# Cross-attention average of a decoder layer: values as stationary 32-column weights in four column groups, divisors by a ones product

## What is computed

```
k, v  = split((ctx @ W_src.T + b_src) * mask)         # ctx: 128 x 512 per sequence
q     = (x1 @ W_tgt.T + b_tgt) * mask                 # 8 heads of 32 channels
attn  = softmax(where(mask, q @ k.T / sqrt(32), -inf))
upd   = attn @ v
x2    = layernorm(x1 + concat([x1, upd]) @ W_out.T + b_out)
```

## Time and profile before

| | us |
|---|---|
| median of three runs | 1570.22 |
| the profiled execution's own time | 1569.91 |
| its span in the trace | 1568.2 |
| PE busy in the span | 1355.5 |
| DVE busy in the span | 915.1 |
| ACT busy in the span | 689.8 |
| GpSimd (POOL) busy in the span | 541.7 |
| `attend`: first weight DMA issued at | 673.01 |
| `attend`: last copy of logits at | 1051.81 |
| `attend`: busy PE from 693.73 to 1014.81, of 321.08 | 314.06 |

### The profile page before, as it was taken

The page is one execution under the profiler, slowest core; times in us unless marked ns, Lnnn a source line. Parts: engine busy times, 40 slices in busy tenths (PEclk is TensorE's granted clock), DMA queues, the critical chain, the costliest instruction groups (busy, mean ns, idle before and its releaser), DMA issues. The chain is left out here.

```text
span 1568.2 us, 24828 instructions
## 1 busy us (share of the span) xinstructions
PE 1355.5 (86%) x8188; PEld 1035.6 (66%) x8189; DVE 915.1 (58%) x1735; ACT 689.8 (44%) x1253; POOL 541.7 (35%) x460
## 2 busy tenths in 40 slices
PE   4889556669999999569999999969979999999995
PEld 1344456658888888358888888855756666666653
DVE  4899759769999999535454445446512212122196
ACT  2545349947777777323433343331022222222214
POOL 2565500014555555522312331211234444444311
PEclk9999878889999999679999999979989999999998
DMA  3698787744333332042232021023021111111164
GB/s 89 149 244 234 207 221 198 216 121 104 95 94 94 94 94 61 14 123 71 85 98 98 31 62 61 28 81 110 0 74 54 57 57 55 56 56 57 59 200 134
DMA packets 147325, 158.20 MB, mean 101 GB/s; under 512 B 63440, under 2 KB 112176, under 8 KB 145712
## 3 DMA queue, kind: packets, MB, share of 16 engines
q1 hardware_dynamic: 134320, 123.63, 27.0%
q0 software_dynamic: 8320, 29.37, 7.3%
q10 hardware_dynamic: 4608, 4.20, 0.8%
HBM read 104.72 MB, written 42.99 MB: 94 GB/s over the span
## 5 line engine op out<-in xcount | busy, mean ns | idle before, releaser
L2531 DVE TENSOR_TENSOR hidden<-unit_psum,gate 128x352 f32<-128x352 f32 x72 | 37.8, 525 | 210.1 <-ACT gate L2494 210.1
L1944 POOL TENSOR_TENSOR scores<-scores,score_max 128x1024 f32<-128x1024 f32 x32 | 60.8, 1899 | 243.2 <-DVE score_max L1872 243.2
L478 PE MATMUL proj_psum<-filtered 128*128 128x512 f32 x192 | 96.0, 648 | 34.8 <-DMA filtered<-in_xT 28.1
L2462 PE MATMUL unit_psum<-wd,hiddenT 128*128 (+1 forms) x432 | 112.0, 395 | 14.2 <-issue 12.9
L549 PE MATMUL proj_psum<-window,toep 128*128 128x128 f32 x512 | 77.2, 319 | 46.8 <-DMA toep<-in_fir 24.3
L2393 POOL DMA_INDIRECT unit_rows<-x_rows,token_of_slot x72 | 69.8, 970 | 126.9 <-PE unit_psum L2436 104.4
L668 ACT ACTIVATE filtered<-proj_psum 32x512 f32<-32x512 f32 x168 | 98.6, 587 | 30.3 <-PE proj_psum L549 26.3
L549 PEld LDWEIGHTS proj_psum<-window,toep 128*128 128x128 f32 x512 | 73.4, 231 | 50.5 <-issue 47.6
L697 DVE SCALAR_TENSOR_TENSOR filtered<-proj_psum,conv_taps,filtered 128x508 f32<-128x508 f32 (+1 forms) x144 | 95.0, 733 | 19.3 <-ACT filtered L596 19.3
L2400 POOL DMA_INDIRECT outs<-unit_out,choice_of_slot x72 | 71.1, 987 | 99.8 <-DVE unit_out L2536 97.1
L2462 PEld LDWEIGHTS unit_psum<-wd,hiddenT 128*128 128x128 f32 (+1 forms) x432 | 76.4, 190 | 37.0 <-issue 29.1
(11 more groups left out here) (286 smaller groups left out, 3258.5 us busy)
## 6 DMA issues: line engine op xcount, KB each, us to landing
toep<-in_fir SPq DMA_DIRECT2D x32, 384.0 KB, 4.0
neg_decay_blocks<-in_gw1s POOLq DMA_DIRECT2D x8, 1280.0 KB, 10.6
ndg<-filtered SPq DMA_DIRECT2D x8, 1024.0 KB, 6.1
neg_decay_gram<-ndg SPq DMA_DIRECT2D x16, 512.0 KB, 3.7
ctxT_tiles<-in_ctxT SPq DMA_DIRECT2D x16, 512.0 KB, 3.6
gathered<-outs SPq DMA_DIRECT2D x32, 256.0 KB, 3.0
window<-value SPq DMA_DIRECT2D x32, 192.0 KB, 4.0
filtered<-in_xT SPq DMA_DIRECT2D x8, 512.0 KB, 7.0
```

The source lines that it names most:

```text
L478: mm = pe.matmul(psum[:, pair_bank(n, p, m % 2), :], wqkv[m // KD][:, k, (m % KD) * 128:(m % KD) * 128 + 128], xT[:, u, k, :], start=(k == ...
L1944: pool.tensor_tensor(sc[:, i % 2, t, :, :], sc[:, i % 2, t, :, :], wide(mx[:, t, :], [128, XH, L], 2), ALU.subtract).then_inc(shifted[t], 1)
L2462: mm = pe.matmul(psum[:, u, DOWN, 0:D], hidT[0:HR[t], u, t, :], M.wd[0:HR[t], bass.ds(chosen["down"], 1), t, :].rearrange("p e n -> p (e n)"),
```

## The change

The product is turned round. The values of a head, 128x32, are now the weights, and the 128x128 probabilities of that head are streamed through them (`update`, lag 2): 16 products of 128 columns for a unit. Head 4k + g writes the 32 PSUM rows of column group g, so that four neighbouring products stand in four column groups, and the result comes out with channels in rows, as `output` wants it. The denominators come from a second product (`divisor`, lag 2): a 128x32 tile of ones as weights, 256 columns of probabilities streamed, eight products for a unit, again over four column groups; it yields each denominator 32 times, one for each channel row. DVE takes the reciprocal of the whole 128x512 bank (`invert_divisor`) and multiplies it with the update's bank straight into `updateT` (`divide`). `turn_update`, `keep_updateT` and both `divide(t)` of before go away. The values lie without the ones column.

The orders of all four engines, the lags and the users of the four banks are new: PE now begins a turn with `queries`, keys and values lie a turn apart, `scores` stands four steps behind `queries`, and `divisor` and `update` end the turn. On DVE `keep_values`, `invert_divisor`, `ln_shift`, `divide` and `keep_queries` follow each other.

```diff
--- before.py
+++ after.py
@@ -1481,12 +1481,12 @@
         qryT = sb("queryT", [128, 2, KD, P * L])
-        val = sb("value_ones", [128, 2, P, XH, XD + 1])
+        val = sb("context_values", [128, 2, P, D])
+        ones = sb("ones_columns", [128, XD])
         sc = sb("scores", [128, 2, P, XH, L])
...
         mx = sb("score_max", [128, P, XH])
-        den = sb("softmax_den", [128, P, XH])
-        upd = sb("update", [128, P, D])
+        inv_den = sb("inverse_divisors", [128, KD * P * L])
         updT = sb("updateT", [128, KD, P * L])
@@ -1499,10 +1499,10 @@
-        USES = ((("keys", 0), ("queries", 0), ("turn_x2", 4)),
-                (("turn_x1", 0), ("output_x1", 0), ("values", 0), ("turn_update", 2)),
-                (("probs10", 2), ("probs00", 2), ("average0", 2), ("router", 4)),
-                (("output", 3), ("probs01", 2), ("probs11", 2), ("average1", 2)))
+        USES = ((("queries", 1), ("keys", 0), ("turn_x2", 4)),
+                (("turn_x1", 0), ("output_x1", 1), ("values", 1)),
+                (("probs10", 2), ("router", 5), ("probs00", 2), ("update", 2)),
+                (("probs11", 2), ("output", 3), ("probs01", 2), ("divisor", 2)))
         BANK = {what: bank for bank, uses in enumerate(USES) for what, _ in uses}
@@ -1519,7 +1519,6 @@
         exp_done = pair("exp_done")
-        den_done = pair("den_done")
         ln_step = signal("att_ln2_step")
@@ -1687,33 +1686,37 @@
-            def average(t):
-                what = f"average{t}"
-                def step(i):
-                    wait_emptied(pe, f"probs{t}0", i)
-                    wait_emptied(pe, f"probs{t}1", i)
-                    wait_emptied(pe, "values", i)
-                    wait_free(pe, what, i)
-                    for h in range(XH):
-                        at = 2 * (h % 4) + h // 4
-                        mm = pe.matmul(bank(what, slice(h * (XD + 1), (h + 1) * (XD + 1))), scT[:, t, at, :],
-                                       val[:, i % 2, t, h, :], start=True, stop=True)
-                    mm.then_inc(filled[BANK[what]], 1)
-                return step
-            def turn_update(i):
-                for t in range(P):
-                    wait_emptied(pe, f"average{t}", i)
-                wait_free(pe, "turn_update", i)
+            def divisor(i):
+                if i == 0:
+                    pe.wait_ge(ones_set, 1)
+                for t in range(P):
+                    for half in range(2):
+                        wait_emptied(pe, f"probs{t}{half}", i)
+                wait_free(pe, "divisor", i)
+                for t in range(P):
+                    for g in range(4):
+                        rows = slice(g * XD, g * XD + XD)
+                        out = psum[rows, BANK["divisor"], :].rearrange("p (k t) -> p k t", k=KD)[:, :, t * L:t * L + L]
+                        mm = pe.matmul(out, ones[:, :], scT[:, t, KD * g:KD * g + KD, :], start=True, stop=True)
+                mm.then_inc(filled[BANK["divisor"]], 1)
+            def update(i):
+                for t in range(P):
+                    for half in range(2):
+                        wait_emptied(pe, f"probs{t}{half}", i)
+                wait_emptied(pe, "values", i)
+                wait_free(pe, "update", i)
                 for t in range(P):
                     for k in range(KD):
-                        at = k * P * L + t * L
-                        mm = pe.transpose(bank("turn_update", slice(at, at + L)), upd[:, t, k * 128:k * 128 + 128], M.ident[:, :])
-                mm.then_inc(filled[BANK["turn_update"]], 1)
+                        for g in range(4):
+                            rows, h = slice(g * XD, g * XD + XD), 4 * k + g
+                            at = k * P * L + t * L
+                            mm = pe.matmul(psum[rows, BANK["update"], at:at + L], val[:, i % 2, t, h * XD:h * XD + XD],
+                                           scT[:, t, KD * g + k, :], start=True, stop=True)
+                mm.then_inc(filled[BANK["update"]], 1)
             def output(i):
-                wait_emptied(pe, "turn_update", i)
+                wait_emptied(pe, "update", i)
                 wait_free(pe, "output", i)
@@ -1741,9 +1744,9 @@
             pe.wait_ge(w_src_in, 16)
-            unrolled(UNITS, (output, 3), (turn_x1, 0), (turn_probs(1, 0), 2), (keys, 0), (turn_probs(0, 1), 2),
-                     (turn_probs(0, 0), 2), (output_x1, 0), (turn_probs(1, 1), 2), (average(0), 2), (average(1), 2),
-                     (queries, 0), (values, 0), (turn_x2, 4), (turn_update, 2), (scores, 0), (router, 4))
+            unrolled(UNITS, (queries, 1), (turn_probs(1, 1), 2), (turn_probs(1, 0), 2), (turn_x1, 0), (scores, 1),
+                     (output, 3), (output_x1, 1), (router, 5), (keys, 0), (turn_probs(0, 1), 2), (turn_probs(0, 0), 2),
+                     (values, 1), (turn_x2, 4), (divisor, 2), (update, 2))
@@ -1784,17 +1787,11 @@
-                    wait_filled(act, f"average{t}", i - 1)
+                    wait_filled(act, "divisor", i - 1)
+                    wait_filled(act, "update", i - 1)
                     act.activation(scT[:, t, 4 * half:4 * half + 4, :].rearrange("p h t -> p (h t)"), bank(what), ACT.Copy
...
                 return step
-            def keep_updateT(i):
-                wait_filled(act, "turn_update", i)
-                wait_filled(act, "output", i - 1)
-                act.activation(updT[:, :, :].rearrange("p k t -> p (k t)"), bank("turn_update"), ACT.Copy
-                               ).then_inc(emptied[BANK["turn_update"]], 1)
@@ -1812,9 +1809,9 @@
-            unrolled(UNITS, (exps(1), 2), (copy_x1, 0), (keep_x2T, 5), (keep_updateT, 3), (keep_x1T, 0), (normalize, 4),
-                     (exps(0), 2), (keep_probs(1, 0), 2), (keep_probs(0, 1), 2), (keep_probs(0, 0), 2),
-                     (keep_probs(1, 1), 2), (keep_keys, 0))
+            unrolled(UNITS, (exps(1), 3), (keep_x2T, 6), (exps(0), 3), (keep_probs(1, 1), 3), (normalize, 5),
+                     (keep_x1T, 1), (keep_probs(1, 0), 3), (keep_probs(0, 1), 3), (copy_x1, 0), (keep_keys, 1),
+                     (keep_probs(0, 0), 3))
@@ -1829,11 +1826,9 @@
-                wait_filled(dve, "average0", i - 2)
-                wait_filled(dve, "average1", i - 2)
-                dve.tensor_tensor(val[:, i % 2, :, :, 0:XD], bank("values").rearrange("p (b h d) -> p b h d", b=P, d=XD),
-                                  wide(b_val[:, :].rearrange("p (h d) -> p h d", d=XD), [128, P, XH, XD], 1),
-                                  ALU.add).then_inc(emptied[BANK["values"]], 1)
+                wait_filled(dve, "update", i - 2)
+                dve.tensor_tensor(val[:, i % 2, :, :], bank("values").rearrange("p (b c) -> p b c", b=P),
+                                  wide(b_val[:, :], [128, P, D], 1), ALU.add).then_inc(emptied[BANK["values"]], 1)
@@ -1872,19 +1867,19 @@
-            def divide(t):
-                what = f"average{t}"
-                def step(i):
-                    wait_filled(dve, what, i)
-                    av = bank(what, slice(0, XH * (XD + 1))).rearrange("p (h d) -> p h d", d=XD + 1)
-                    dve.reciprocal(den[:, t, :], av[:, :, XD]).then_inc(den_done[t], 1)
-                    dve.wait_ge(den_done[t], i + 1)
-                    wait_filled(dve, "turn_update", i - 1)
-                    dve.tensor_tensor(upd[:, t, :].rearrange("p (h d) -> p h d", d=XD), av[:, :, 0:XD],
-                                      wide(den[:, t, :], [128, XH, XD], 2), ALU.mult).then_inc(emptied[BANK[what]], 1)
-                return step
+            def invert_divisor(i):
+                wait_filled(dve, "divisor", i)
+                wait_emptied(dve, "update", i - 1)
+                dve.reciprocal(inv_den[:, :], bank("divisor")).then_inc(emptied[BANK["divisor"]], 1)
+            def divide(i):
+                wait_filled(dve, "update", i)
+                wait_emptied(dve, "divisor", i)
+                wait_filled(dve, "output", i - 1)
+                dve.tensor_tensor(updT[:, :, :].rearrange("p k t -> p (k t)"), bank("update"), inv_den[:, :],
+                                  ALU.mult).then_inc(emptied[BANK["update"]], 1)
@@ -1922,12 +1917,11 @@
-            dve.memset(val[:, :, :, :, XD:XD + 1], 1.0).then_inc(ones_set, 1)
-            dve.wait_ge(ones_set, 1)
+            dve.memset(ones[:, :], 1.0).then_inc(ones_set, 1)
             dve.wait_ge(weights_in, 7 * 16)
-            unrolled(UNITS, (masks, 0), (max_scores(1), 1), (max_scores(0), 1), (keep_residual, 0), (divide(0), 2),
-                     (keep_queries, 0), (divide(1), 2), (keep_values, 0), (ln_shift, 3), (scale_scores(0), 0),
-                     (keep_logits, 4), (residual, 2), (scale_scores(1), 0), (statistics, 2))
+            unrolled(UNITS, (masks, 0), (max_scores(0), 1), (keep_values, 1), (invert_divisor, 2), (ln_shift, 3),
```

(4 more changed lines are left out.)

## The result

The changed kernel takes 1542.45 us (median of four runs, 1539.77 to 1544.88) against 1571.51 us of the kernel before in the same measurements: a ratio of 0.982, 95% interval 0.980 to 0.984. The forecast was 1541, within 1520 to 1566. The profiled execution's span went from 1568.2 to 1538.1 us.

What follows compares the result with a forecast made beforehand. PE, busy 21.11 of each 21.55 us turn, was taken to set the pace. Shorter turns (16.7 us) and no clock falls (12.0) gave 28.7 off 1569.9: 1541.2 us, range 1520 to 1566.

Steps and rivals of the forecast that it cites:

- Removed, 4.66 us per unit of PE: On PE per unit: average 3.50, turn_update 0.56 and the wait for DVE's emptying of values 0.60 go, 4.66 us.
- the wait behind turn_x2: On PE, about 0.60 us before turn_update, waiting for the bank that DVE empties of values; claimed to go.
- Added on PE, 2.15: On PE per unit: update 1.10 and divisor 1.05 us, with products overlapping by four, as scores shows for row groups.
- rival 3: On PE: column groups do not overlap in float32, 6.9 us; kernel 1601, or 1589 without clock falls; chance 0.14.
- The reciprocal, 3.37: On DVE: the 128x512 reciprocal takes 3.37 us, from the line through three sizes, 8, 20 and 32 elements.
- The eight repeats: On DVE: a skill page's divide repeating eight times, eight times 0.68, would make the reciprocal 5.4 us; not taken.
- The wait, 1.32: PE waits 1.32 us a turn: DVE needs 5.53 us after divisor before scores, PE has 4.21 of work.
- the forecast's chain of 5.53 us: On DVE after divisor: reciprocal 3.37, ln_shift 0.15, multiply 0.68, keep_queries 0.88 and hand-overs, 5.53 us until scores can start.
- The turns, 14 x 1.19 = 16.7: Between scores 0 and 15: a turn of 20.36 against 21.55 us, 1.19 gained in each of 14, 16.7 us.
- The clock, 12.0: In the steady turns: all seven falls to 1.2 GHz after average go, 7 x 1.71 = 12.0 us gained.
- Rival 1: In the new turn's loose stretch of waits, transposes and scores: the clock falls stay, kernel 1553 us; chance 0.18.
- The emptying of the pipeline, nothing: At the stage's end: 3.50 + 0.56 go and 5.10 us come, taken as no change, 2 us either way.

## Why the prediction was right

**Removed, 4.66 us per unit of PE.** Right. The steps that stayed have the lengths of the earlier trace rows within 0.1, and the wait behind turn_x2 is gone (0.53 there now).

**Added on PE, 2.15.** Right in kind, 0.27 too high: 0.89 + 0.99 = 1.88. Start-up was costed at 0.2 a step, after scores, and is 0.03 and 0.13 (against 3.45 / 4). PE's own work is 18.98 us a turn, shown bare by the run with the short reciprocal, where 19.04 was forecast. That the overlap carries the change is shown: without it the kernel is slower than before. It was rival 3's mechanism at 7.06 us, inside its bounds of 6.9 to 7.4, and it comes out at 1598 between that rival's 1589 and 1601. "TensorE: Matmul & The Clock Gate" in the Trainium skill (Part 3) has 2.38-fold for three column tiles. The 3.6- to 3.9-fold of four groups here goes the same way and comes nearer to the number of groups.

**The reciprocal, 3.37.** Right: 3358 ns. The line through 8, 20 and 32 elements held up to 512, and its half, 256 columns, took 1.76. The eight repeats of "VectorE: DVE Perf Modes" in the Trainium skill would have given an estimate of 5.4; the measurement decides for 6.3 ns per element.

**The wait, 1.32.** Right in size: 0.93 ahead of probs11 and 0.37 ahead of probs10 in the timeline, 1.30 by the difference of the turns 20.28 and 18.98 where only the reciprocal was shortened. The cause, the reciprocal, is right too. The last link is not: the forecast's chain of 5.53 us ended with keep_queries ahead of scores, and no wait stands there. The chain ends with the multiply ahead of probs10, and PE's own probs10 and turn_x1 (0.99 us) follow before scores. They are about as long as the keep_queries and hand-over that were costed, so that the sum came out the same; that part is luck. That the chain is long by what PE lacks in cover, and not DVE short of time, is shown from the other side too: turn_x2 (0.53 us of PE work) moved under it gave 0.43 back, and half of the reciprocal moved away took the wait away whole.

**The turns, 14 x 1.19 = 16.7.** Measured 17.8: 309.3 us of the old kernel without falls of the clock, less 291.5.

**The clock, 12.0.** Right: no fall in 15 turns, and 11.8 us with the old kernel's averages set apart. Rival 1, falls that stay in the loose end of the new turn, did not happen.

**The emptying of the pipeline, nothing.** 2.1 us longer; it was given 2 either way. The forecast set what goes and what comes for one unit against each other. In both traces two units are left in this stretch, each with its own average, or its own divisor, reciprocal and update. The clock's share in the two stretches, 0.85 and 0.89, was left out too.

**Ahead of the first scores.** The forecast has no term for it. This stretch became 2.7 us shorter. In all seven kernels with the new order it takes 11.7 to 18.7 us, in both with the old order 20.7 and 20.8. So it goes with the new order; how much of its length is the load of weights, no run tells. That the 2.7 us here and the 2.1 of the emptying nearly cancel is luck.

## What to carry over

When work is moved from the engine that sets the pace to one with slack, the busy times tell little: find the chain from the moved work back to the first engine and put the cover beside it, step by step. A chain that is a little too long is best cut where a part of its input is ready early, and moved into the idle time ahead of it. Look at the granted clock in windows before costing a step: here a sparse step cost more than its own length shows, and setting a dense step in its middle gave that back.

## What the runs showed of the hardware

Float32 products in four column groups of the array overlap 3.6- to 3.9-fold, 32 records of 128 columns in 0.99 us against 3.58 in one group. The overlap stands two products (four records) in a row for one group without loss worth the name (1.04 us) and mostly goes with four products (2.36 us); three were not tried, and why it goes is not shown. VectorE's reciprocal takes 202 ns for 8 elements and 3358 for 512, with 6.3 ns for each element more at all sizes between. The granted clock fell seven times in 15 turns, each time after 3.5 us of products of 33 columns. It did not fall with two stretches of 1.7 us of them on either side of a 1.8 us step of 256-column products, nor with 7 us of products in one column group, 128 or 256 columns each.
